# Causal attention's first score pass without mask products: VectorE adds the mask in place before it takes the maximum

## What is computed

```
scores = jnp.einsum('bhqd,bhkd->bhqk', q, k) * scale          # q, k after rotary embedding
scores = jnp.where(causal, scores, jnp.finfo(jnp.float32).min)
ex = jnp.exp(scores - jnp.max(scores, axis=-1, keepdims=True))
attn = ex / (jnp.sum(ex, axis=-1, keepdims=True) + 1e-08)
o = jnp.einsum('bhqk,bhkd->bhqd', attn, v)
```

## Time and profile before

| what | us |
|---|---|
| median of 3 runs | 2159.39 (2157.69 to 2160.56) |
| profiled run, whole | 2168.65 |
| its span | 2166.8 |
| first row block's reduction starts | 44.25 |
| first key-major product starts | 90.08 |
| last row block's reduction starts | 347.7 |

### The profile page before, as it was taken

How to read it: one execution, slowest core, us unless ns; L and a number is a source line. 1 busy time by engine, 2 the same in 40 slices (tenths; PEclk the granted TensorE clock), 3 DMA queues, 4 the chain that set the end, 5 groups by cost and what they waited for, 6 DMA issues and landing times. The chain is left out here.

```text
span 2166.8 us, 68261 instructions
## 1 busy us (share of the span) xinstructions
PE 1926.3 (89%) x26493; PEld 1299.6 (60%) x26493; DVE 1729.9 (80%) x3617; ACT 1502.6 (69%) x2952; POOL 1264.4 (58%) x1132
## 2 busy tenths in 40 slices
PE   5788888678999999999999999999999999983283
PEld 2333333236777777777777777777777777762162
DVE  4666664378999999999999999999999999834713
ACT  2156656357888888888788888888888888854123
POOL 4500000277778777877787778777787778712053
PEclk8699999689999999999999999999999999996587
DMA  6412100201111112111211113111311111101512
GB/s 155 118 44 46 24 3 2 71 28 32 40 33 42 32 51 73 41 32 42 83 41 32 41 32 92 36 38 31 92 41 32 34 39 42 32 21 39 186 37 70
DMA packets 70612, 108.18 MB, mean 50 GB/s; under 512 B 20887, under 2 KB 47774, under 8 KB 68734
## 3 DMA queue, kind: packets, MB, share of 16 engines
q1 hardware_dynamic: 68262, 100.87, 16.3%
q0 software_dynamic: 1280, 2.62, 0.4%
q10 hardware_dynamic: 752, 0.33, 0.1%
HBM read 41.60 MB, written 12.26 MB: 25 GB/s over the span
## 5 line engine op out<-in xcount | busy, mean ns | idle before, releaser
L1730 POOL TENSOR_TENSOR qk<-rot_cos,rot_sin 128x512 f32<-128x512 f32 x256 | 324.7, 1276 | 86.6 <-DVE rot_sin L1476 86.4
L1740 POOL TENSOR_TENSOR qk<-qk,rnorm 128x512 f32<-128x512 f32 x256 | 263.2, 1044 | 139.3 <-DVE rnorm L1509 139.3
L1474 DVE TENSOR_TENSOR rot_cos<-pA,layer_tab 128x512 f32<-128x512 f32 x384 | 262.2, 683 | 29.6 <-ACT sq L1258 21.6
L437 ACT ACTIVATE probs_by_key<-pT 128x512 f32<-128x512 f32 (+3 forms) x384 | 177.0, 489 | 155.5 <-PE pT L320 120.8
L1486 DVE TENSOR_REDUCE sumsq<-sq 128x8 f32<-128x512 f32 x384 | 256.8, 670 | 30.5 <-ACT sq L1258 30.5
L502 DVE TENSOR_REDUCE minus_max<-pS 128x1 f32<-128x1024 f32 (+7 forms) x256 | 184.4, 753 | 110.4 <-PE pS L290 109.6
L1476 DVE TENSOR_TENSOR rot_sin<-pA,layer_tab 128x512 f32<-128x512 f32 x384 | 260.4, 678 | 0.0
L1258 ACT ACTIVATE sq<-pA 128x512 f32<-128x512 f32 x384 | 231.3, 602 | 30.6 <-PE pA L880 23.9
L1316 ACT ACTIVATE probsT<-pD 64x512 f32<-64x512 f32 x384 | 226.3, 589 | 6.3 <-PE pD L925 4.1
L880 PE MATMUL pA<-W_ahead,x_feature_major 128*128 128x512 f32 x384 | 203.7, 614 | 17.8 <-DVE rot_sin L1476 11.7
L880 PE MATMUL pA<-layer_weights,x_feature_major 128*128 128x512 f32 x384 | 197.5, 596 | 0.1
(11 more groups left out here) (318 smaller groups left out, 4555.9 us busy)
## 6 DMA issues: line engine op xcount, KB each, us to landing
v_shifted<-v SPq DMA_DIRECT2D x96, 384.0 KB, 3.5
v_shifted<-v SPq DMA_DIRECT2D x95, 128.0 KB, 3.4
q_stack<-stacked SPq DMA_DIRECT2D x24, 192.0 KB
k_stack<-stacked SPq DMA_DIRECT2D x24, 192.0 KB
W_ahead<-in_Wqkv_dram SPq DMA_DIRECT2D x12, 384.0 KB
layer_weights<-in_Wqkv_dram SPq DMA_DIRECT2D x12, 384.0 KB
stacked<-part SPq DMA_DIRECT2D x32, 128.0 KB, 2.4
tokens_in<-tokens SPq DMA_DIRECT2D x2, 1024.0 KB
```

The source lines that it names most:

```text
L437: act.activation(PTr[n % RING][:, 0:q1 - q0], ST[n % 2][:, 0:q1 - q0], AF.Exp, scale=float(AD) ** -0.5).then_inc(exp_done, 1)
L1474: dve.tensor_tensor(t1[c % 2][:, :].rearrange("p (h g d) -> p h g d", g=2, d=32), a, tabl[s % 2][:, j].unsqueeze(1).broadcast_to([P, 8, 2, ...
L1730: pool.tensor_tensor(qk(s, c), t1[c % 2][:, :], t2[c % 2][:, :], ALU.add).then_inc(added[c], 1)
L1740: pool.tensor_tensor(v, v, rn[p % 2][:, o:o + 8].unsqueeze(2).broadcast_to([P, 8, DH]), ALU.mult).then_inc(scaled[c], 1)
```

## The change

The product with the mask (L290) goes; the last score product counts up `s_ready` itself. VectorE, once the scores are ready, adds the mask table to the diagonal block where it lies in PSUM, waits on a new semaphore `hidden` for that addition, and then reduces as before. Once, at the first block, it waits for the table to be loaded. The mask products of the second pass (L320) stay.

```diff
@@ row_block
                 for c in range(0, n, 512):
-                    pe.matmul(S[at % 2][:, c:min(n, c + 512)], QS[r][0:STACK, h, qt * P:n],
-                              KS[r][0:STACK, h, c:min(n, c + 512)], start=True, stop=True, skip_group_check=True)
-                pe.matmul(S[at % 2][:, n - P:n], identb[:, :], cm[:, 0, :], start=False, stop=True, skip_group_check=True)\
-                    .then_inc(s_ready, 1)
+                    mm = pe.matmul(S[at % 2][:, c:min(n, c + 512)], QS[r][0:STACK, h, qt * P:n],
+                                   KS[r][0:STACK, h, c:min(n, c + 512)], start=True, stop=True, skip_group_check=True)
+                mm.then_inc(s_ready, 1)
@@ largest
                 c = u // TB * TB + TURNS[u % TB]
+                n = (TURNS[u % TB] + 1) * P
+                if (g, u) == (0, 0):
+                    dve.wait_ge(mask_in, 16)
+                dve.tensor_tensor(S[at % 2][:, n - P:n], S[at % 2][:, n - P:n], cm[:, 0, :], ALU.add).then_inc(hidden, 1)
+                dve.wait_ge(hidden, NS * g + u + 1)
                 dve.tensor_reduce(NM[:, c:c + 1], S[at % 2][:, 0:(TURNS[u % TB] + 1) * P], AX.X, ALU.max, negate=True).then_inc(s_free, 1)
```

## The result

| | before | after |
|---|---|---|
| median, us | 2159.97 (2157.69 to 2168.3, 4 runs) | 2210.39 (2204.89 to 2237.35, 4 runs) |
| ratio after / before | | 1.0235 [1.0185, 1.0286] |
| profiled run, whole, us | 2168.65 | 2204.89 |
| its span, us | 2166.8 | 2203.1 |
| mean granted clock of that span (1.0 is 2.4 GHz) | 0.939 | 0.923 |

The kernel became slower, as forecast, but by 50 us between the medians and 36 us between the profiled runs, where 13.4 was forecast; the time lies above the range.

The account below looks back on a forecast made before the run. No engine was taken as saturated: two score and two key-major buffers tie three engines into one chain. First pass 5.5, rest of iteration 1 0.5, steady iterations 6.0, end 0.2, clock 1.2: +13.4, 2172.8 us; range 2162 to 2187.

Parts of the forecast that it names:

- one more fall: One further drop of TensorE's granted clock in a steady iteration, behind the splits of the maxima: +1.2 us.
- the rest of the sum: All forecast terms but the clock: first pass, rest of iteration 1, steady iterations, end of iteration 7; 12.2 us.
- Rival 2: Slower by much: dearer addition or wait (d about 0.5), 2183 us, or a clock fall every iteration, 2180; chance 0.15.
- Length of the addition: VectorE adding the mask to 128 columns in PSUM takes 0.29 us, bounded by 0.19 and 0.42.
- The wait: VectorE's reduction, waiting on its own semaphore, starts 0.03 to 0.04 us after the addition ends.
- d: Extra VectorE time per row block from the addition and its wait: 0.33 us, 84 us in all.
- GpSimd doesn't disturb the addition: In iteration 0, the addition's PSUM and SBUF inputs avoid slowing beside a busy GpSimd; nothing added.
- First pass: Chain to the first key-major product: 22 longer reductions less 21 removed mask products, +5.5 us.
- Steady heads: Heads after an iteration's first: one addition on the path less four mask products; +0.09, +0.19, +0.09 us.
- The first head: First head of a steady iteration: late split of the maxima and two additions on the path, less four masks; +0.64 us.
- The mask product at 0.06 us: Each removed 128-column TensorE product gives back 0.06 us at the full clock; 0.107 us was taken at 1.2 GHz.
- Everything behind 349 us simply moves: After 349 us no row block is left, so earlier loss only shifts the later work.

Follow-up runs that it names:

- e8: The changed kernel, program unchanged, measured again on chip 1: 2206.99 us, 1.0195 against the kernel before.
- e1: The changed kernel with TensorE's mask products left in beside VectorE's additions on every block: 2207.59 us, 1.0158 against the kernel before.
- e2: No mask in the first pass, neither products nor additions: 2186.29 us, 1.0066 against the kernel before.
- e9: No additions; two mask products on blocks of 128, 768, 640, 512 columns, none on the others: 2160.39 us, 0.9979 against the kernel before.
- e10: The changed kernel plus two mask products on each block of 128, 768, 640 and 512 columns: 2200.36 us, 1.0153 against the kernel before.
- e3 padded: The change for the first 32 row blocks alone, with 64 already-met waits ahead in TensorE's stream: 2184.75 us, 1.0078 against the kernel before.
- e4: VectorE masks the odd row blocks (128, 256, 384, 512 columns), TensorE the even ones: 2172.98 us, 1.0029 against the kernel before.
- e5: From group 1 on, VectorE masks only 1024-column blocks and each group's first 896-column block, TensorE all others: 2243.74 us, 1.0326 against the kernel before.
- e3: The change for group 0 alone (32 row blocks), mask products everywhere else, no padding: 2214.86 us, 1.0183 against the kernel before.

## Why the prediction was wrong

**The sign was right, the size wrong, and the step that failed is the clock: +1.2 us for one more fall.** By the line above, the 99 us more at the lower clock over ten runs of after are worth 36 us (0.365 x 99; for the six of e8 beside before on their chip it is 89 us, worth 32), and the rest of the sum, forecast at 12.2 us, came out at 7.5. In the profiled pair it is 28 us (0.365 x 77) and 8 of the 36. Rival 2 held the mechanism in its second half, a fall in every iteration. But it priced a fall at 1.2 us, where the falls were twice as long as the one read from the earlier trace rows (6.8 against 3.4 us) and, if the rest of the first head went by forecast, cost 2.0 to 2.4 each. It had nothing for the low stretch of 34 us in iteration 7 nor for the longer one at the start, and only a chance of 0.15. The place was named, behind the splits of the maxima, and so was the section of the Trainium skill ("TensorE: Matmul & The Clock Gate", "A second HAM failure mode: psum-queue depth-cycling") on an engine that idles between groups as it cycles through PSUM buffers; the trace of after agrees, with a fall of 6.8 us in the first head of each of four iterations (3 to 6). I then counted one event, though nothing made the one iteration different from the others.

**The cause has two halves, and I had only one.** The waits for VectorE alone (e1): +37 us at the lower clock, against before on the same chip. The missing products alone (e2): +63. Both (after, in e8): +89. e9 and e10 show the second half from the other side, by putting the products back.

Point by point:

- Length of the addition: forecast 0.29 us, measured 0.29 to 0.30. The wait: forecast 0.03 to 0.04, measured 0.03. d = 0.33, right. The statement of the Trainium skill ("VectorE: DVE Perf Modes", "The DRAIN you can't avoid") that a semaphore between two instructions costs nothing did not hold for this pair, 0.03 us after the end with the wait against 0.09 before the end without.
- GpSimd doesn't disturb the addition: right, 300 ns at most. But the split of the maxima in iteration 0, whose instructions read SBUF alone, had three of its four instructions at 1.2 us instead of one (and a second at 0.63), with GpSimd at work beside it both times, and took 4.0 us instead of 2.8 from its first instruction to the next row block's. I had read the one slow instruction of it and not asked whether a shifted split would meet GpSimd more. The timeline of after:

```profile
79.48 1.20 DVE L516 TENSOR_TENSOR max_left<-minus_max,max_parts 128x32 f32<-128x32 f32 x1
80.71 1.18 DVE L518 CAST max_parts<-max_left 128x32 bf16<-128x32 f32 x1
81.92 1.19 DVE L520 TENSOR_TENSOR max_parts<-max_left,max_parts 128x32 bf16<-128x32 f32 x1
```

- First pass: forecast +5.5 to the first key-major product, measured +7.4. 1.2 of the excess is this split; 0.7 is left unexplained. e3 padded, with the change up to block 31, had block 44 at 95.56 us, 6.2 later than before.
- Steady heads: forecast +0.09, +0.19, +0.09, measured at the full clock +0.04, +0.21, +0.03. Four mask products on the path, one addition of eight on it: right, and e4 (additions with room cost nothing) and e5 (one without room: +0.27) confirm it one by one. The first head, forecast +0.64, never ran at the full clock in after; it took 11.9 to 12.3 us against 9.17, with a fall of 6.8 us each, so this term is untested.
- The mask product at 0.06 us: right in the heads of e2 (0.23 to 0.30 shorter, for four on the path), and the very reading that hid its other use.
- "Everything behind 349 us simply moves": right for after, and by luck. It took 512 instructions out of TensorE's stream; e3 and e5 took out 64 and 70, and there the unchanged layers lost time that the padding gave back.
- Waits: forecast longer for VectorE, shorter for ScalarE. Over 100 to 348 us they went from 37.1 to 39.6 us and from 52.6 to 45.6, and VectorE's own wait for scores from 79.0 to 30.5:

```profile
PEld pT L317 <- ACT probs_by_key L437: 45.6, 96, 1.6
PEld pS L289 <- DVE minus_max L507: 39.6, 61, 1.4
...
DVE pS L505 <- PE pS L289: 30.5, 46, 2.4
```

- The range: it held the falls of rival 2 at half of their price as the upper end. The kernel before itself had stretches of 41 and 20 us at the lower level, so the trace showed that the clock can stay down once it has fallen. Six falls at 1.2 us and one more stretch of 41 us, at the price of 0.37 us measured since, come to 2195 us; the range should have reached that far, and the result lies above even that.

What stays open: why a fall is sometimes short and sometimes 20 to 34 us long, with the same code in each iteration (the 34 us lay in iteration 7 in the profiled run of after and in iteration 3, from 172.9 us, in that of e8); the 0.7 us; and how far the relation of time and low clock, fitted across runs of before, holds for kernels with another chain, beyond the heads of 15.26 us.

## What to carry to other kernels

In a stretch where TensorE runs at its full clock with several engines tied in one chain, ask of each edit not only what it puts on the chain but what it does to the clock: small products that hide beside other work cost little and may hold it up, and any new wait may drop it. Count a fall once for each time the pattern repeats, and let the upper end of the range hold at least one stretch as long as the longest that the trace shows. And when a change in one stage makes an untouched stage slower, compare the lengths of the instruction streams before looking for a mechanism: padding is a one-line experiment. When two kernels were measured on different chips, compare each with the kernel before on its own chip, as the lower clock's share differs between chips.

## What the runs showed of the hardware

- Taking 256 products of 128 columns out of a stage and adding nothing lowered the mean clock from 0.939 to 0.925 (same chip) and made the kernel slower, 1.0066 [1.0036, 1.0097].
- 70 satisfied waits ahead of a stage took a kernel from 1.0326 [1.0281, 1.037] to 1.0111 [1.0051, 1.017], by moving the code behind it. TensorE's unexplained waits there, 24 before and 5 after the padding, all stood at the same place modulo 256 of its stream.
- At the lower clock a microsecond cost this kernel 0.37 us by the line of 55 runs, and 0.36 to 0.39 by the heads that ran wholly at that level, less than the half that it would cost if TensorE's rate set the time at the full clock too.
- An addition by VectorE that reads and writes 128 columns of PSUM and reads 128 of SBUF took 0.30 us, no more than by the rate of 256 and 512 columns that go to SBUF (1.02 ns a column).
